# Parts of three attentions' preparation made between the units of the first heads' first pass

## What is computed

```python
x = x + own_attention(layernorm(x))        # 16 heads of 16, causal, keys and values with a gated part
x = x + cross_attention(layernorm(x), ctx) # 16 heads, rotary, causal mask
x = x + feed_forward(layernorm(x))
x = x + second_attention(layernorm(x))     # 16 heads, not causal
x = x + wide_attention(layernorm(x), ctx)  # one head of 256
x = x + experts(layernorm(x))              # 16 experts, the best two, and a shared one

# own attention
k_enh = k + kv_gate * gram_gate * k_geo
v_enh = v + kv_gate * gram_gate * v_geo
scores = einsum('bhtd,bhsd->bhts', q, k_enh) * SCALE   # masked, softmax
out = einsum('bhts,bhsd->bhtd', attn, v_enh)
```

## Time and profile before

| | us |
|---|---|
| median of three runs | 3462.88 |
| lowest, highest | 3462.72, 3467.68 |
| the profiled execution | 3462.7 |
| its span, first to last instruction | 3461.4 |

### The profile page before, as it was taken

The page is one execution under the profiler, slowest core; times in us unless marked ns, Lnnn a source line. Parts: engine busy times, 40 slices in busy tenths (PEclk is TensorE's granted clock), DMA queues, the critical chain, the costliest instruction groups (busy, mean ns, idle before and its releaser), DMA issues.

```text
span 3461.4 us, 46823 instructions
## 1 busy us (share of the span) xinstructions
PE 3253.9 (94%) x17732; PEld 1740.7 (50%) x17732; DVE 2340.6 (68%) x4347; ACT 1783.5 (52%) x2551; POOL 544.0 (16%) x990
## 2 busy tenths in 40 slices
PE   4999989999999988999999988999999999899999
PEld 3544443368744443337864544333786444433477
DVE  4874578746686568865678557785667854788555
ACT  1464636653346454674344655466434555546632
POOL 0101010014211101002511120100240111010033
PEclk8998989999999998999999989899999999989999
DMA  3222011103121201202312120111131202012023
GB/s 134 38 38 43 2 28 28 20 30 118 51 47 35 39 1 29 38 10 63 112 36 45 26 38 1 37 29 34 54 108 41 38 16 39 1 37 38 10 81 94
DMA packets 118101, 147.74 MB, mean 43 GB/s; under 512 B 25384, under 2 KB 75920, under 8 KB 117596
## 3 DMA queue, kind: packets, MB, share of 16 engines
q1 hardware_dynamic: 117876, 144.74, 17.4%
HBM read 74.25 MB, written 4.46 MB: 23 GB/s over the span
## 4 chain that ended last, share of the span: by engine, by line
PE 78%; DVE 12%; ACT 4%; issue 2%; SPq 1%; DMA 0%; POOL 0%; DVEq 0%; ACTq 0%
PE psum L1777 17%; PE psum L670 14%; PE psum L615 12%; PE psum L638 12%; PE psum L927 7%; DVE small L744 3%; PE psum L480 2%; PE psum L866 2%; PE psum L679 2%; SPq L789 1%; ACT work L710 1%; PE psum L461 1%; PE psum L856 1%; PE psum L642 1%; PE psum L1603 1%
## 5 line engine op out<-in xcount | busy, mean ns | idle before, releaser
L744 DVE TENSOR_REDUCE small<-psum 128x1 f32<-128x512 f32 (+6 forms) x1856 | 1143.3, 657 | 252.8 <-PE psum L615 216.0
L710 ACT ACTIVATE work<-psum 128x1024 f32<-128x1024 f32 (+5 forms) x1024 | 921.1, 935 | 469.3 <-PE psum L642 242.5
L615 PE MATMUL psum<-work 96*128 96x512 bf16 (+4 forms) x2688 | 711.1, 332 | 34.7 <-DVE small L744 12.8
L1777 PE MATMUL psum<-rounded_work 128*128 128x512 f32 x2592 | 602.2, 394 | 9.9 <-DVE rounded_work L1863 6.5
L638 PE MATMUL psum<-work 99*128 99x512 bf16 (+4 forms) x2048 | 580.5, 367 | 10.4 <-DMA work<-work 8.5
L1777 PEld LDWEIGHTS psum<-rounded_work 128*128 128x128 f32 x2592 | 490.4, 190 | 115.8 <-DVE rounded_work L1863 8.3
L670 PE MATMUL psum<-work 128*32 128x512 f32 (+4 forms) x4480 | 535.8, 531 | 1.6 <-ACT work L710 1.4
L615 PEld LDWEIGHTS psum<-work 96*128 96x128 bf16 x2688 | 238.6, 101 | 578.8 <-DVE small L744 366.6
L638 PEld LDWEIGHTS psum<-work 99*128 99x128 bf16 (+1 forms) x2048 | 182.6, 99 | 201.9 <-ACT work L710 56.4
L1878 ACT CAST rounded_work<-work 128x512 fp32r<-128x512 f32 x144 | 89.4, 621 | 342.0 <-DVE work L1919 318.6
L776 POOL CAST small<-small 128x16 bf16<-128x16 f32 x96 | 18.8, 196 | 1326.1 <-issue 949.9
(11 more groups left out here) (287 smaller groups left out, 3809.0 us busy)
## 6 DMA issues: line engine op xcount, KB each, us to landing
work<-work SPq DMA_DIRECT2D x320, 192.0 KB, 4.3
work<-combine SPq DMA_DIRECT2D x64, 512.0 KB, 4.1
work<-in_w_gate SPq DMA_DIRECT2D x64, 128.0 KB, 3.5
work<-in_w_up SPq DMA_DIRECT2D x64, 128.0 KB, 3.4
work<-in_w_down SPq DMA_DIRECT2D x64, 128.0 KB, 3.8
work<-in_x SPq DMA_DIRECT2D x8, 512.0 KB, 5.6
out<-x SPq DMA_DIRECT2D x8, 512.0 KB, 2.9
work<-work SPq DMA_DIRECT2D x64, 28.9 KB, 2.0
```

Of the source, the lines that this page charges most:

```text
L615: ins = nc.tensor.matmul(dst[:, c * n:(c + 1) * n], A.q_pair[0:ROWS, slot, h, P * i:P * (i + 1)], A.k_of(pair, h)[0:ROWS, s0:s0 + n], star ...
L710: nc.scalar.activation(probs[0:size, n % 4, :, 0:P * many], banks(2 * (n % 2), 2)[0:size, :, 0:P * many], ACT.Exp, scale=DH ** -0.5).then_ ...
L744: nc.vector.tensor_reduce(tops[:, pair % 2, places[0]:places[-1] + 1:step], src, AX.X, ALU.max) \
L1777: ins = nc.tensor.matmul(dst, a_parts[i], b_parts[j], start=start and n == 0, stop=stop and n == 2, skip_group_check=True)
```

## The change

Own stage. `attention_plan` gets a list `beside` of pieces that are put behind a given unit of the first pass. Behind unit 4 (counted from 0) come the gates (TensorE's turning, `gates_tensor`, and VectorE's `gate_vector`), behind unit 22 the low and doubling of queries 1, behind 25 and 28 the rests of the two halves of keys 1 (VectorE) with their middle parts (ScalarE), behind 31 and 34 their lows, with the doubling of keys 1 at the end. The first unit no longer waits for the gate; the first score does. The twelve busy matmuls go. ScalarE's values and casts are in another order.

Second stage. The eight value blocks (TensorE) and their copies (ScalarE) stand behind units 1, 3, ..., 15 of the first pass; they use four banks in turn. The first unit waits for the last rest, the first score for the last values. VectorE doubles only keys 0 and queries 0, each one unit earlier than before; Pool doubles keys 1 and queries 1. ScalarE makes the middle part of unit 3 right behind its high part. SyncE loads the keys and the queries of pair 0 first, then those of pair 1 and pair 2.

```diff
-def attention_plan(keys, causal, lead, extra):
+def attention_plan(keys, causal, lead, extra, beside):
...
     firsts[-1] += [("join", PAIRS_OF_HEADS - 1), ("cut", PAIRS_OF_HEADS - 1)]
+    for unit, piece in beside:
+        firsts[unit].append(piece)
...
-        heads = {A.tag: A for A in (Heads("own", FULL, True, 11, q_pair, slot_keys, V, [("context", n) for n in range(KD + 1)]),
+        heads = {A.tag: A for A in (Heads("own", FULL, True, 11, q_pair, slot_keys, V, [("context", n) for n in range(KD + 1)],
+                                          [(4, ("late", "gates", 0)), (22, ("late", "queries", 1)), (25, ("late", "rest", 2)), (28, ("late", "rest", 3)),
+                                           (31, ("late", "low", 2)), (34, ("late", "low", 3))]),
...
-                                    Heads("second", FULL, False, 10, q_pair, slot_keys, V, [("wide", n) for n in range(4)]))}
+                                    Heads("second", FULL, False, 10, q_pair, slot_keys, V, [("wide", n) for n in range(4)],
+                                          [(2 * i + 1, ("late", "values", i)) for i in range(NT)]))}
...
                     if n == 0:
                         pe.wait_ge(*at("minus_ones_landed", a))
+                        if a == "own":
+                            pe.wait_ge(*at("gate_ready"))
+                        elif a == "second":
+                            pe.wait_ge(*at("values_ready_second", NT - 1))
...
                 keys_ready(0)
                 load_keys(A, 0)
-                load_keys(A, 1)
                 queries_ready(0)
                 load_queries(A, 0)
-                load_queries(A, 1)
-                load_keys(A, 2)
-                load_queries(A, 2)
+                for pair in (1, 2):
+                    load_keys(A, pair)
+                    load_queries(A, pair)
...
             key_gate_scalar(0)
             key_gate_scalar(1)
+            values_scalar(2, 3)
             keys_high(0)
+            values_scalar(3, 4)
             keys_high(1)
-            values_scalar(2, 4)
+            keys_middle(0)
+            keys_middle(1)
             key_gate_scalar(2)
             key_gate_scalar(3)
-            keys_middle(0)
-            keys_middle(1)
-            values_scalar(4, 6)
+            values_scalar(4, NT)
             keys_high(2)
             keys_high(3)
-            values_scalar(6, NT)
-            keys_middle(2)
-            keys_middle(3)
...
         def gated_banks_free(queue):
-            queue.wait_ge(*at("gate_ready"))
             queue.wait_ge(*at("values_copied", NT - 1))
...
+        def second_values_tensor(i):
+            if i < 4:
                 pe.wait_ge(*at("second_rest", i))
-                project(bank(i)[:, 0:D], lambda k: x_tile("feed", i, k), resident["qkv1"][:, :, 2 * D:3 * D]).then_inc(*up("second_values", i))
+            else:
+                pe.wait_ge(*at("values_ready_second", i - 4))
+            project(bank(i % 4)[:, 0:D], lambda k: x_tile("feed", i, k), resident["qkv1"][:, :, 2 * D:3 * D]).then_inc(*up("second_values", i))
...
-                if n:
+                if n not in (0, 4):
                     second_middle(n - 1)
...
+                if n % 4 == 3:
+                    second_middle(n)
...
-                if n in (4, 6):
-                    second_doubles(n // 2 - 2)
-            second_doubles(2)
-            second_doubles(3)
...
         def second_banks_free(queue):
-            queue.wait_ge(*at("values_ready_second"))
+            queue.wait_ge(*at("second_rest", len(second_units) - 1))
...
-            pe.wait_ge(*at("values_copied", 5))
-            busy_tensor(12, value_banks[5])
             heads_tensor(own_heads, gated_banks_free)
```

More of the change, by code:

```diff
@@ L561, in build_program, with __init__ @@
         class Heads:
-            def __init__(self, tag, keys, causal, lead, q_pair, k_of, V, extra=()):
+            def __init__(self, tag, keys, causal, lead, q_pair, k_of, V, extra=(), beside=()):
                 self.tag, self.keys, self.causal = tag, keys, causal
@@ L565, in __init__ @@
                 self.ns, self.nk = len(keys), sum(keys)
-                self.units, self.steps, self.plan = attention_plan(keys, causal, lead, list(extra))
+                self.units, self.steps, self.plan = attention_plan(keys, causal, lead, list(extra), beside)
                 order = [(pair, s, part) for kind, *key in self.plan if kind == "score" for pair, s, part in [key[1:]]]
@@ L694, in heads_tensor @@
                     ins.then_inc(*up("out_spun", a, *key))
+                elif kind == "late":
+                    what, n = key
+                    if what == "gates":
+                        gates_tensor()
+                    elif what == "values":
+                        second_values_tensor(n)
                 elif kind == "context":
@@ L727, in heads_scalar @@
                     nc.scalar.copy(oT[:, k, HALF * half:HALF * (half + 1)], bank(ring[(kind, *key)][0])).then_inc(*up("out_turned", a, *key))
+                elif kind == "late":
+                    what, n = key
+                    if what == "rest":
+                        keys_middle(n)
+                    elif what == "values":
+                        second_values_scalar(n)
                 elif kind == "context":
@@ L762, in heads_vector @@
                     nc.vector.tensor_tensor(out, src[:, :, :, 0:DH], spread(over, 3, DH), ALU.mult).then_inc(*up("normalised", a, pair))
+                elif kind == "late":
+                    what, n = key
+                    if what == "gates":
+                        gate_vector()
+                    elif what == "queries":
+                        queries_low(n)
+                    elif what == "rest":
+                        keys_rest(n)
+                    elif what == "low":
+                        keys_low(n)
                 elif kind == "wide":
@@ L1148, in gated_vector @@
                 nc.vector.tensor_tensor(q_raw[:, :, k], q_raw[:, :, k], in_halves(0, k), ALU.subtract).then_inc(*up("queries_rest", k))
-            for k in range(KD):
-                dve.wait_ge(*at("queries_middle", k))
-                own(nc.vector.tensor_tensor(in_halves(2, k), q_raw[:, :, k], in_halves(1, k), ALU.subtract), "queries_cut", k)
-                double_queries(k, "queries_doubled", k)
+            queries_low(0)
             keys_full(0)
@@ L1156, in gated_vector, with queries_low, gate_vector @@
             keys_rest(1)
[L1157 removed]
             keys_low(0)
             keys_low(1)
+            keys_full(2)
             keys_full(3)
[L1161 to L1164 removed]
+        def queries_low(k):
+            dve.wait_ge(*at("queries_middle", k))
+            own(nc.vector.tensor_tensor(in_halves(2, k), q_raw[:, :, k], in_halves(1, k), ALU.subtract), "queries_cut", k)
+            double_queries(nc.vector, k, "queries_doubled", k)
+        def gate_vector():
             dve.wait_ge(*at("gates_turned"))
@@ L1474, in second_tensor, with second_values_scalar @@
                 project_turned(bank(n), resident["qkv1"][:, :, second_parts[name][0]], k, "feed", half).then_inc(*up("second_projected", n))
-            for i in range(NT):
+        def second_values_tensor(i):
+            if i < 4:
                 pe.wait_ge(*at("second_rest", i))
-                project(bank(i)[:, 0:D], lambda k: x_tile("feed", i, k), resident["qkv1"][:, :, 2 * D:3 * D]).then_inc(*up("second_values", i))
+            else:
+                pe.wait_ge(*at("values_ready_second", i - 4))
+            project(bank(i % 4)[:, 0:D], lambda k: x_tile("feed", i, k), resident["qkv1"][:, :, 2 * D:3 * D]).then_inc(*up("second_values", i))
+        def second_values_scalar(i):
+            act.wait_ge(*at("second_values", i))
+            nc.scalar.copy(V_heads[:, i], bank(i % 4)[:, 0:D].rearrange("p (h d) -> p h d", d=DH)).then_inc(*up("values_ready_second", i))
         def second_scalar():
@@ L1483, in second_scalar @@
                 nc.scalar.activation(half_of(cut[:, parts[0]], k, half), bank(n), ACT.Identity, bias=resident[bias][:, k:k + 1]).then_inc(*up("second_high", n))
-                if n:
+                if n not in (0, 4):
                     second_middle(n - 1)
-            second_middle(len(second_units) - 1)
-            for i in range(NT):
-                act.wait_ge(*at("second_values", i))
-                ins = nc.scalar.copy(V_heads[:, i], bank(i)[:, 0:D].rearrange("p (h d) -> p h d", d=DH))
-            ins.then_inc(*up("values_ready_second"))
+                if n % 4 == 3:
+                    second_middle(n)
         def second_middle(n):
```

49 lines of the change are left out of this document (26 added, 23 removed).

## The result

| | before | changed |
|---|---|---|
| median of twelve runs each, us | 3464.25 | 3473.99 |
| lowest, highest | 3456.67, 3469.04 | 3467.92, 3478.01 |
| first profiled execution, span | 3462.7, 3461.4 | 3478.01, 3476.7 |

The changed kernel is slower: the ratio is 1.0029, 95% interval 1.0020 to 1.0037, some 10 us, where 5 us faster was forecast and 3471 was the end of the range. The table adds up this second pair by stage, four items together, from the starts of the first unit (U) and the first score (S) of each attention in TensorE's timeline. "Forecast" is the prediction's own sum. The last column has the differences of the first pair.

A forecast was written before the change was run, and what follows sets the result against it. TensorE's own work (78% of the chain of waits) bounds the kernel, VectorE the prefixes before the first scores. Own stage +0.5 and second stage -5.6 gave -5.1 us: 3457.6 us, range 3446 to 3471.

The forecast's parts named there:

- Own start, first score: Own stage: units start 5.6 us earlier, prefix gets +2.5, +2.2, +0.7; first score -0.2 us per item.
- What they guarded is the clock: Own stage: removing twelve busy matmuls costs 0, the prefix clock being low before too; bound 1.7 us per item either side.
- A: Stretch from start or second stage's first score to own first score, four items together: -2.7 us.
- Behind the first score: Own stage, after its first score: VectorE's leftover work costs +0.8 us per item, ends 0 and +2.9.
- VectorE's debt: Own stage: VectorE still owes 2.9 us behind the first score (a rest, two lows, one doubling), partly hidden.
- Second stage, start: Second stage: queries' loads issued earlier land at 490.9, so the first unit runs then, before at 495.50.
- Second stage, prefix: Second stage, first unit to first score: value blocks between units and low clock (+1.5) lengthen it, +12.8 us over four items.
- D: Stretch from the second stage's first unit to its first score, four items together: +12.8 us.
- C: Stretch from cross attention's first score to the second stage's first unit, four items together: -18.4 us.
- slower, by the own stage: Rival, chance 0.13: own stage absorbs none of 2.9 us, scores begin at half clock; own +15.7, second -5.6: 3472.8 us.
- B: Stretch from own first score to cross attention's first unit, four items together: +3.2 us.
- two of four cases: Skill page on cold matmuls after DMA waits: trace agrees in two of four; by it second stage -4.8 for -5.6.

The follow-up runs named there:

- second pair: Second profiled execution of the kernel before and of the changed kernel, code unaltered: 3462.03 and 3472.79 us.
- first pair: First profiled execution of the kernel before and of the changed kernel: 3462.7 and 3478.01 us.
- e10: Changed kernel with twelve busy matmuls ahead of the own stage's first unit and fourteen ahead of the second's: 3459.06 us, ratio 0.9982.
- e13: Kernel before with eight more unread matmuls in each of two feed stage waits: 3453.9 us, ratio 0.9964.
- e14: Changed kernel with eight more unread matmuls in each of two feed stage waits: 3458.32 us, ratio 0.9980.
- e7: Kernel before with only the second stage's part, plus fourteen unread matmuls in its wait for the loads: 3453.7 us, ratio 0.9974.
- e4: Kernel before with only the second stage's part, value blocks 0 to 2 ahead of its first unit: 3452.01 us, ratio 0.9962.
- e1: Kernel before with only the own stage's part of the change: 3471.05 us, ratio 1.0018.
- e3: Changed kernel with the twelve busy matmuls back ahead of the own stage's first unit: 3471.49 us, ratio 1.0017.
- e6: Changed kernel with gates ahead of the own first unit, five own pieces later, three value blocks ahead of the second's: 3445.85 us, ratio 0.9952.
- e11: Changed kernel, own gates ahead, five pieces behind units 38 to 66, three value blocks ahead of second stage's first unit: 3441.59 us, ratio 0.9934.

## Why the prediction was wrong

- *Own start, first score.* Forecast -0.2 per item: items two to four had -0.05, -0.21 and -0.23. **Right**, with the 2.5 us of VectorE behind unit 5 (2.25), and with the prefix longer by 5.4 us in each (22.7 to 22.9 for 17.3 to 17.4; forecast 2.5 + 2.2 + 0.7). The queries' second half did not meet Pool: in item two of the first execution Pool's gating of the values was over at 988.92 and VectorE's low of queries 1 began at 990.14. Item one failed: forecast -2.1, measured +2.9 (+1.3 in the first pair, where item three had +5.3). The step that failed is "What they guarded is the clock. In the prefix it was low in all four items before too ... so I put the difference at 0". The premise is right and the conclusion does not follow, since it matters what work the low clock falls on: here on gates that VectorE stands waiting for, and on the first scores. Gates priced at 3.5 us took 6.8 at half clock, in one or two items: +5 in the sum, +9 in the first pair. Without that (`e10`) A was -1.0.
- *Behind the first score.* Forecast +0.8 per item, as VectorE's debt; measured +1.0, +1.8, +0.7, +1.8. The number is near for another reason: VectorE's debt was absorbed without a wait of TensorE (8.00 us busy of 8.00 in all four items). The cost is the clock, 0.65 to 0.67 in those 8 us for 0.79, 1.00, 0.71 and 1.00, which the forecast had as a bound of 1.7 and took at 0: +2.2 in the sum.
- *Second stage, start.* From the start of the projections to the first unit before 23.07 and 21.37 us, after 19.06 and 17.41: -4.0, forecast -4.6, so 2.7 us of the sum. The queries were ready when forecast, 14.76 us behind the projections' start in item one (14.67 forecast), though the doubling's second copy took 1.37 for 0.42 beside Pool. The term that was too small is the load: taken at 3.8 us from its issue, the queries' loads took 4.2 to 4.4 in item one.
- *Second stage, prefix.* Forecast +3.2 per item with a low clock nearly always; measured +3.3 in two items and +4.0 in two. The low clock was there in all of them, and it was priced too low: 1.5 per item, where D fell by 2.0 per item once it was gone (114.0 in the changed kernel, 105.9 in `e10`).
- *What no step had:* ahead of the projections C was 4.8 us longer than before, of which the projections' own clock gave 1.7 back. The code is the same there. The low clock in the feed stage is the larger part, since with fillers in that stage (`e13`, `e14`) the 4.8 are gone. The forecast took every stretch outside the two places as fixed. It had read the clock 0.50 in items one and three and 1.00 in items two and four at one such place and put a price on that place alone.
- Of the rivals, "slower, by the own stage" came out nearest in time (3472.8 for 3473.99), but that is luck: the scores did begin at half clock, but nothing of the 2.9 us was owed, and the second stage, which it had at -5.6, gave nothing.

In short, the second pair is 16 us off the forecast's sum: 5.2 in A, 2.2 in B, 5.7 in C, 1.8 in D and 1.2 behind them, and for this last no run shows a cause.

What stays open: why the clock falls ahead of the gates in item one of all five executions, once in item three and never in two and four, behind waits of the same length, and how much of the 8 to 10 us that `e7` and `e4` gained in stages that they do not touch is that clock. Only the waits of the feed stage and of the two entries were filled. Two executions of each kernel do not show either whether the change makes the low clock of the feed stage more frequent, or whether those two happened to have it: single profiles of `e1`, `e3` and `e10` have it in all four items too, those of `e6` and `e11` in two.

A page of the Trainium skill, "TensorE: Matmul & The Clock Gate", section "HAM oscillation — how this bites in real kernels", warns of matmuls that start cold behind a wait for a DMA. In the second stage the traces agree in five of eight items of the two changed executions, where the clock was at 0.50 from 0.8 to 0.9 us ahead of the first unit. In the other three it fell 1.4 to 1.6 us behind the first unit, which still took 0.38 us. The first block ran at half clock in all eight (1.63 to 1.92 us for 1.03), and in none of the four items of `e7` and of `e10`, whose waits were filled. The prediction had taken its "two of four cases" from a gap at another place. In the own stage the same kind of wait was followed by gates at half clock in three of the eight items.

## What to carry to other kernels

When work that keeps TensorE busy is moved out of a wait, price what comes behind the wait at both clocks, and leave enough of it there: three value blocks of 0.88 us kept in the load's wait turned +0.26% into -0.38%. Work of the engine that bounds a prefix lengthens it by its whole length when it is moved into it (5.4 us here); behind the prefix, pieces far apart cost less than pieces close together (`e11` for `e6`, B lower by 2.8 us). And before a difference of 0.3% is laid to an edit, sum the stages that it does not touch, from two executions of each kernel.

## What the runs showed of the hardware

Behind the same wait of 1.97 us, in the same code, the clock held in two items and fell in two of one execution of the kernel before; where it fell it stayed low through the sixteen spreads in one item (3.57 us) and was back ahead of them in the other (2.05). Eight extra matmuls of 0.22 us in each of two such waits, which nobody reads, made the kernel before 0.36% faster. Fourteen in the wait of 3.4 us for a load took the half clock off the matmuls behind it (1.03 us for 1.72). The turning of the gates, 32 matmuls, took 3.64 us at full clock and 6.84 at half clock. A copy by VectorE of 128x1024 bfloat16 elements took 1.37 us beside an operation of Pool and 0.42 where Pool was idle. One kernel's executions spread over 3456.1 to 3476.8 us in 33 runs, and the longer they took, the lower the mean granted clock (0.959 to 0.949, correlation -0.96).
